# The sum of the normed residual and the gated row: VectorE in SBUF in place of TensorE in a bank

## The chip, the cores and the metric

One core of one Trainium2 chip runs the whole program in one launch. The metric is the device time of the program in microseconds; a profiled execution has a time of its own and, a little below it, the span from its first to its last record. TensorE is called PE here, VectorE DVE, ScalarE ACT, GpSimd POOL and SyncE SP.

## What is computed

Eight examples of 512 tokens by 512 features pass through two blocks of attention and feed-forward. Only the last lines of the last feed-forward and its residual matter here:

```python
for _ in range(K_STEPS):                    # 4 steps, on one row per example
    t = layer_norm(thought, pn_gamma, pn_beta)
    t = jax.nn.gelu(t @ d1_w + d1_b, approximate=False)
    thought = thought + (t @ d2_w + d2_b)
broadcast = (thought @ bc_w + bc_b)[:, None, :]
gate = jax.nn.sigmoid(x @ gate_w + gate_b)
out = x + gate * broadcast
return layer_norm(out, out_gamma, out_beta)
...
x = x + _layernorm(_L1_ffn_ref(_layernorm(x, axis=-1), ...), axis=-1)
```

The inner `x` is the layer norm of the residual: the "normed residual". `gate * broadcast` is the "gated row".

## The kernel before

Everything up to the last feed-forward runs example by example, software-pipelined over the engines, and takes the first 3705 us. For each example it leaves the residual x3 and the sigmoid gate in DRAM, and the moments of the residual in SBUF (`pd_moments`, `pd_rstd`).

The output stage takes the rest. It works on tiles of 128 tokens by 512 features, f32: `NF` = 32 tiles, four per example, in a written-out software pipeline. Each engine has its own loop, and only semaphores tie them together. `fin_place(k)` gives the two SBUF places of tile k, the residual and the gate; the second is overwritten step by step and is at last what goes out. Per tile k:

- SP loads residual and gate of a whole example (`fin_load`), three examples ahead at most.
- PE spreads the row of the example over 128 partitions of a bank (`fin_row`, L2416, once per example; banks P0, Y0, O).
- ACT makes `fin_h`, the normed residual, from residual, rstd and shift (`fin_first`, L1366), three tiles ahead; it has four places and waits for the sum of tile k - 4.
- DVE multiplies row and gate in place: the gated row (L1962).
- PE adds the two: a matmul of `fin_h` by an identity and one of the gated row by an identity into the same bank, E0 or E1 in turn (L2427, L2428). The f32 matmuls have two records each in the trace.
- DVE takes the statistics of the sum from the bank (L1944, L1949 through `fin_measure` and `fin_aggregate`), and writes (sum - mean) * gamma to SBUF (L1981).
- POOL makes rstd from the variance (L1074, L1076).
- DVE multiplies by rstd and adds beta (L1967), and takes the statistics of that (L1944, L1949).
- POOL makes the second rstd and a shift (L1074, L1076, L1088, L1090), ACT applies them in place (L1374), and POOL adds the residual (L1095). SP stores the tile (L882).

DVE's loop has `NF + 2` turns; in turn k it does the first step of tile `new` = k, the middle ones of `mid` = k - 1 and the last ones of `old` = k - 2. Its order within a turn is L1962 (new), L1967 (old), L1944 (mid), row work, L1944 (old), L1949 (mid), L1949 (old), L1981 (mid), row work. POOL's turn is rstd of one tile, rstd and shift of the one before, and L1095 of the one before that.

The rows of the first seven examples are done when the stage begins. That of the last one is not, and its four steps are woven into the first turns: `rows_work(1, p)` is called with p = 2k and 2k + 1 in turn k on DVE and PE, and nearby on ACT and POOL, and a table (`ROWS_DVE`, `ROWS_PE`) says what falls on which p. A step takes 12 of them, six turns: norm (DVE: L1737, L1742, L1744), T (PE, L2295, 8 small matmuls), "in" (DVE, L1764), d1 in two halves (PE, L2307, 16 matmuls each), "bias" (DVE, L1772), Gelu (ACT), tr (PE, L2314), "hid" (DVE, L1775), d2 in two halves (PE, L2319, 32 in all), "part" (DVE, L1778), a sum (PE, L2325), "add" (DVE: L1781, L1783, L1731, L1733), and a small rstd on POOL. PE's queue is in order: the sum of tile k stands ahead of the row work of p = 2k.

Of the kernel before, what the change touches and what calls it, by code (L numbers as in the profile page):

```python
# [5 lines left out]
ALU = mybir.AluOpType  # L6
# [299 lines left out]
def build(nc, x, raw_f, raw_i, gate_scale, up_scale, down_scale, rope1_tables, causal, identity_b,  # L306
# [8 lines left out]
    with ExitStack() as ctx:  # L315
# [15 lines left out]
        ident, k_dec = ident_dec[:, 0:P], ident_dec[:, P:P + 2 * H0].rearrange("p (c h) -> p c h", c=2)  # L331
# [10 lines left out]
        stats, moments = sb("stats", [P, NL, 6]), sb("moments", [P, NL, 2])  # L342
# [80 lines left out]
        gam, bet = X[1][:, 3, :], y_acc[:, 3, :]  # L423

        def row_const(n):
# [11 lines left out]
        fin_h = sb("fin_h", [P, 4, D], c=G)  # L437
# [5 lines left out]
        ps = {n: pairs_[n[0]][:, int(n[1]), :] if n[0] in "TE" else ctx.enter_context(nc.psum_tensor("ps_" + n, [P, 512], F32))  # L443
              for n in BANKS}
# [158 lines left out]
        NF = NB * NT  # L603
# [4 lines left out]
        fin_h_done, fin_w = count("fin_h", NF), count("fin_w", NF)  # L608
        fin_gated, fin_sum, fin_scaled, fin_affine, fin_out = (count("fin_" + k, NF) for k in ("gated", "sum", "scaled", "affine", "out"))
# [1 line left out]

        fin_moments, fin_rstd = ([Count(s_[k].sem, NF, after=NB * NT) for k in ("xa", "pa")] for s_ in (ln_moments, ln_rstd))
        fin_shift2 = count("fin_shift2", NF)
        BC_BANKS, SUM_BANKS = ("P0", "Y0", "O"), ("E0", "E1")

        def fin_place(k):

            b, t = divmod(k, NT)
            return (xr[:, t, :], y1[:, t, :]) if b == NB - 1 else tuple(fin_ring[b % FIN_RING][:, e, t, :] for e in range(2))
# [771 lines left out]
        def _(dve):  # L1391
# [549 lines left out]
            def fin_measure(k, m, src, need):  # L1941
                n = m * 4 + k % 4
                dve.wait_ge(*need)
                dve.bn_stats(stats[:, n, :], src).then_inc(*fin_stats[m].hit(k))  # L1944
# [6 lines left out]
            for k in range(NF + 2):  # L1951
                new, mid, old = k, k - 1, k - 2
                if new < NF:
                    b, t = divmod(new, NT)
                    z = fin_place(new)[1]
                    if t == 0:
                        dve.wait_ge(*fin_bc.need(b))
                        if b < NB - 1:
                            dve.wait_ge(*fin_in[b % FIN_RING].need(b // FIN_RING))
                    if b == NB - 1:  # L1960
                        dve.wait_ge(*gate_done.need(b, t))
                    dve.tensor_tensor(z, ps[BC_BANKS[b % FIN_RING]][:, :], z, ALU.mult).then_inc(*fin_gated.hit(new))  # L1962
                if 0 <= old < NF:
                    n, z = old % 4, fin_place(old)[1]
                    dve.wait_ge(*fin_scaled.need(old))
                    dve.wait_ge(*fin_rstd[0].need(old))
                    dve.scalar_tensor_tensor(z, z, rstd[:, n:n + 1], bet, ALU.mult, ALU.add).then_inc(*fin_affine.hit(old))  # L1967
                if 0 <= mid < NF:
                    fin_measure(mid, 0, ps[SUM_BANKS[mid % 2]][:, :], fin_sum.need(mid))
                if new < NF:  # L1970
                    rows_work(1, 2 * new)
                if 0 <= old < NF:
                    fin_measure(old, 1, fin_place(old)[1], fin_affine.need(old))
                if 0 <= mid < NF:
                    fin_aggregate(mid, 0)
                if 0 <= old < NF:
                    fin_aggregate(old, 1)
                if 0 <= mid < NF:
                    n, z = mid % 4, fin_place(mid)[1]
                    dve.wait_ge(*fin_moments[0].need(mid))  # L1980
                    dve.scalar_tensor_tensor(z, ps[SUM_BANKS[mid % 2]][:, :], moments[:, n, 0:1], gam, ALU.subtract, ALU.mult)\  # L1981
                        .then_inc(*fin_scaled.hit(mid))
                if new < NF:
                    rows_work(1, 2 * new + 1)

        @block.tensor
        def _(pe):
# [3 lines left out]
            def fill(bank, emptied):  # L1991

                if bank in empties:
                    pe.wait_ge(*empties[bank])
                empties[bank] = emptied
                return ps[bank]
# [333 lines left out]
            for n in range(NB + 1):  # L2330
# [44 lines left out]
                for s in range(SLOTS):  # L2375
# [8 lines left out]
                    if c >= 0:  # L2384
# [8 lines left out]
                        if 0 <= t < NT:  # L2393
# [3 lines left out]
                            dst = fill(OB[t % 2], y_copy.need(c, t))  # L2397
# [23 lines left out]
            for k in range(NF):  # L2421
                if k == NF - NT:
                    fin_row(NB - 1)
                pe.wait_ge(*fin_h_done.need(k))
                pe.wait_ge(*fin_gated.need(k))
                dst = fill(SUM_BANKS[k % 2], fin_scaled.need(k))
                pe.matmul(dst[:, :], ident[:, :], fin_h[:, k % 4, :], start=True, stop=False)  # L2427
                pe.matmul(dst[:, :], ident[:, :], fin_place(k)[1], start=False, stop=True).then_inc(*fin_sum.hit(k))  # L2428
                if k % NT == NT - 1 and k // NT + FIN_RING < NB - 1:
                    fin_row(k // NT + FIN_RING)  # L2430
                for p in (2 * k, 2 * k + 1):
                    rows_work(1, p)
# [112 lines left out]
```

## Time and profile before

| | us |
|---|---|
| median of 3 runs (lowest to highest) | 3875.98 (3874.77 to 3876.49) |
| the profiled execution | 3875.49 |
| its span | 3873.6 |
| PE busy in the span | 3614.9 (93%) |
| DVE busy | 2558.6 (66%) |
| ACT busy | 1502.3 (39%) |
| POOL busy | 1501.3 (39%) |

Shares are averages over the whole span. In the output stage, less than a twentieth of it, the balance of the engines is another one, so it has to be read by itself. A record's length runs from its start to its end; on DVE the next operation can start some 0.08 us before the end of the one before, so work is counted from start to start. An operation that is held up after it was issued shows the time in its own length, not as idle time before it.

### The profile page before, as it was taken

The numbers are of one execution on the slowest core, as the hardware profiler recorded it, in microseconds if no ns is written. First come the engines' busy times: TensorE is split into PE (matmuls) and PEld (weight loads), VectorE is DVE, ScalarE is ACT, GpSimd is POOL, SyncE is SP. The second block draws the span as 40 slices with busy tenths as digits, with TensorE's granted clock in tenths as the row PEclk, the third lists the DMA queues.
The fourth block names the chain that finished last, engine by engine and source line by source line (L and its number), as shares of the span: only waits on it lengthen the run. The fifth ranks groups of instructions, "written<-read, shape, count | busy, mean of one in ns | idle before, by whom it ended". The sixth has DMA issues, their size and how long they took to land.

```text
span 3873.6 us, 51710 instructions
## 1 busy us (share of the span) xinstructions
PE 3614.9 (93%) x18752; PEld 2656.7 (69%) x18752; DVE 2558.6 (66%) x4102; ACT 1502.3 (39%) x2327; POOL 1501.3 (39%) x1846
## 2 busy tenths in 40 slices
PE   6878999999999999999999999999999999978787
PEld 5756786687767886687767786687767786654432
DVE  6755677567764776567765776567765777467568
ACT  5523434434242534434243434344243434314323
POOL 3421562246323552245323552255223552231237
PEclk9989999999999999999999999999999999978888
DMA  6567533254324533353335433454325442350232
GB/s 248 182 223 283 193 124 142 101 216 157 131 104 171 188 116 141 127 205 136 133 108 195 164 140 117 152 187 143 139 88 211 142 159 87 120 187 23 77 112 106
DMA packets 173800, 579.03 MB, mean 149 GB/s; under 512 B 14727, under 2 KB 14983, under 8 KB 168174
## 3 DMA queue, kind: packets, MB, share of 16 engines
q1 hardware_dynamic: 169854, 568.38, 40.8%
q10 hardware_dynamic: 3696, 7.34, 0.5%
q8 instruction: 153, 2.51, 0.3%
q14 instruction: 97, 0.79, 0.1%
HBM read 490.21 MB, written 84.93 MB: 148 GB/s over the span
## 4 chain that ended last, share of the span: by engine, by line
PE 59%; DVE 23%; issue 7%; POOL 5%; ACT 3%; DMA 3%; SPq 0%; DVEq 0%; ACTq 0%; POOLq 0%
PE ps_P L2019 21%; PE ps_Y L2019 9%; PE ps_E L2019 6%; PE ps_O L2019 4%; PE ps_O L2256 4%; PE ps_T L2225 3%; PE ps_T L2019 2%; PE ps_E L2239 2%; DVE roped L1451 2%; DVE pf L1513 2%; DVE row_max L1656 2%; DVE ps_T L1649 2%; DVE stats L1417 1%; DVE roped L1445 1%; POOL X L910 1%
## 5 line engine op out<-in xcount | busy, mean ns | idle before, releaser
L2019 PE MATMUL ps_P<-XnT_hi,w_ring 128*128 128x512 f32 x3328 | 1071.4, 403 | 42.3 <-DVE hf L1676 10.7
L2019 PEld LDWEIGHTS ps_P<-XnT_hi,w_ring 128*128 128x128 f32 x3328 | 600.1, 189 | 211.6 <-issue 77.3
L2019 PE MATMUL ps_P<-XnT_lo,w_ring 128*128 128x512 f32 x1664 | 653.6, 393 | 0.0
L1036 POOL TENSOR_TENSOR hT_lo<-hf,hT_hi 128x512 fp32r<-128x512 f32 x128 | 164.8, 1287 | 871.4 <-ACT hT_hi L1100 871.4
L1252 ACT ACTIVATE probs<-ps_E 128x1024 f32<-128x1024 f32 x320 | 328.2, 1026 | 395.3 <-PE ps_E L2239 394.8
L917 POOL TENSOR_TENSOR pT_lo<-pf,pT_hi 128x512 fp32r<-128x512 f32 x256 | 346.4, 1365 | 302.4 <-ACT pT_hi L1100 302.4
L1656 DVE TENSOR_REDUCE row_max<-ps_T 128x2 fp32r<-128x768 f32 (+3 forms) x448 | 399.9, 916 | 11.0
L1649 DVE TENSOR_TENSOR ps_T<-ps_T,mask 128x512 f32<-128x512 f32 (+1 forms) x320 | 188.1, 588 | 301.3 <-PE ps_T L2225 299.5
L2019 PEld LDWEIGHTS ps_P<-XnT_lo,w_ring 128*128 128x128 f32 x1664 | 314.5, 189 | 69.8
L2019 PE MATMUL ps_Y<-w_big,hT_hi 128*128 128x512 f32 x848 | 312.8, 414 | 13.3 <-POOL hT_lo L1036 7.7
L928 POOL TENSOR_TENSOR sines<-swapped,sinT 128x512 f32<-128x512 f32 x160 | 224.8, 1405 | 172.2 <-ACT swapped L1100 166.0
L1100 ACT ACTIVATE pT_hi<-pf 128x512 fp32r<-128x512 f32 x256 | 161.5, 632 | 289.7 <-DVE pf L1513 289.5
L1100 ACT ACTIVATE swapped<-ps_P 64x512 f32<-64x512 f32 x320 | 189.8, 593 | 188.0 <-PE ps_P L2019 106.2
L972 POOL TENSOR_SCALAR_AFFINE_SELECT probs<-probs 128x512 f32<-128x512 f32 x256 | 159.6, 638 | 239.8 <-ACT probs L1252 238.9
L1513 DVE TENSOR_TENSOR pf<-ps_T,dec 128x512 f32<-128x512 f32 x256 | 172.4, 688 | 119.3 <-POOL pT_lo L917 100.6
L2019 PEld LDWEIGHTS ps_Y<-w_big,hT_hi 128*128 128x128 f32 x848 | 159.0, 187 | 81.5 <-issue 16.4
L2225 PE MATMUL ps_T<-KT,QT 64*128 64x256 f32 (+3 forms) x1024 | 164.5, 379 | 42.1 <-DVE row_max L1656 40.5
L2019 PE MATMUL ps_Y<-w_big,oT_hi 128*128 128x512 f32 x512 | 171.9, 397 | 10.7 <-DVE y_acc L1490 6.3
L1666 DVE SCALAR_TENSOR_TENSOR silu<-silu,ps_P 128x512 f32<-128x512 f32 x128 | 87.5, 684 | 141.3 <-ACT silu L1346 141.3
L1445 DVE TENSOR_TENSOR roped<-ps_P,cosT 128x512 f32<-128x512 f32 x160 | 109.7, 685 | 105.0 <-ACT swapped L1100 104.7
L1451 DVE TENSOR_TENSOR roped<-roped,sines 128x512 f32<-128x512 f32 x160 | 158.3, 990 | 24.0 <-POOL sines L928 24.0
L2019 PE MATMUL ps_O<-w_big,oT_hi 128*128 128x512 f32 x512 | 168.9, 391 | 0.0
(319 smaller groups left out, 7401.6 us busy)
## 6 DMA issues: line engine op xcount, KB each, us to landing
w_ring<-split_dram SPq DMA_DIRECT2D x412, 512.0 KB, 3.4
w_big<-split_dram SPq DMA_DIRECT2D x64, 2048.0 KB, 7.6
dec<-decay SPq DMA_DIRECT2D x32, 1024.0 KB, 5.1
split_dram<-w_ring SPq DMA_DIRECT2D x58, 512.0 KB, 4.5
split_dram<-w_big SPq DMA_DIRECT2D x36, 512.0 KB, 4.4
wo1w<-split_dram SPq DMA_DIRECT2D x8, 2048.0 KB, 7.7
gatew<-split_dram SPq DMA_DIRECT2D x7, 2048.0 KB, 11.0
X<-raw_f SPq DMA_DIRECT2D x46, 256.0 KB, 5.1
```

Of the source, the lines that this page charges most:

```text
L917: pool.tensor_tensor(pT[1][:, k % 4, :], pf[:, k % 2, :], pT[0][:, k % 4, :].bitcast(F32), ALU.subtract).then_inc(*p_lo.hit(n, g, k))
L928: pool.tensor_tensor(sines[:, u % 2, :], swapped[:, u % 2, :], sinT[:, :], ALU.mult)\
L972: pool.affine_select(out=corner, in_=corner, compare_op=ALU.is_ge, fill=0.0, base=0, pattern=[[0, 4], [1, P]], channel_multiplier=-1).then ...
L1036: pool.tensor_tensor(hT[1][:, m % IC, :], hf[:, m % 2, :], hT[0][:, m % IC, :].bitcast(F32), ALU.subtract).then_inc(*h_lo.hit(n, m))
L1100: return act.activation(out_, in_, ACT.Copy)
L1252: act.activation(dst[:, heads_of(ns), :].rearrange("p (b n) i -> p b n i", n=len(ns)), psE[:, :, :].rearrange("p b (n i) -> p b n i", n=le ...
L1451: dve.tensor_tensor(roped[:, u % 3, :], roped[:, u % 3, :], sines[:, u % 2, :], ALU.add)\
L1513: dve.tensor_tensor(out_, in_, table, ALU.mult).then_inc(*p_f.hit(n, g, pf_at(g, k)))
L1649: dve.tensor_tensor(corner.rearrange("p b n (k s) -> p b (n k) s", s=P) if nh == 1 else corner, corner.rearrange("p b n (k s) -> p b (n k) ...
L1656: last = dve.reduce_max(row_max[:, g % 2, block, heads_of(ns)].rearrange("p (b n) -> p b n", n=len(ns)), psT[:, :, at:at + len(ns) * w].re ...
L2019: last = pe.matmul(dst, stat[s_], mov[m_], start=first_ and k == 0, stop=last_ and k == n - 1, **kw)
L2225: last = pe.matmul(dst[q][:, at + m * w:at + (m + 1) * w], QT[rows_, g % 3, pair, cols(block)], KT[rows_, g % 3, 0:w], start=True, stop=True)
```

## The change

PE no longer makes the sum and has no bank for it. DVE adds `fin_h` to the gated row in place, in the same turn as L1962, behind L1967. The statistics (L1944) and L1981 read the sum from SBUF. The semaphore `fin_sum` is now raised by DVE; ACT's wait for it stays.

```diff
-        BC_BANKS, SUM_BANKS = ("P0", "Y0", "O"), ("E0", "E1")
+        BC_BANKS = ("P0", "Y0", "O")
...
                     dve.scalar_tensor_tensor(z, z, rstd[:, n:n + 1], bet, ALU.mult, ALU.add).then_inc(*fin_affine.hit(old))
+                if new < NF:
+                    dve.wait_ge(*fin_gated.need(new))
+                    dve.wait_ge(*fin_h_done.need(new))
+                    dve.tensor_tensor(fin_place(new)[1], fin_h[:, new % 4, :], fin_place(new)[1], ALU.add).then_inc(*fin_sum.hit(new))
                 if 0 <= mid < NF:
-                    fin_measure(mid, 0, ps[SUM_BANKS[mid % 2]][:, :], fin_sum.need(mid))
+                    fin_measure(mid, 0, fin_place(mid)[1], fin_sum.need(mid))
...
                     dve.wait_ge(*fin_moments[0].need(mid))
-                    dve.scalar_tensor_tensor(z, ps[SUM_BANKS[mid % 2]][:, :], moments[:, n, 0:1], gam, ALU.subtract, ALU.mult)\
+                    dve.scalar_tensor_tensor(z, z, moments[:, n, 0:1], gam, ALU.subtract, ALU.mult)\
                         .then_inc(*fin_scaled.hit(mid))
...
-                pe.wait_ge(*fin_h_done.need(k))
-                pe.wait_ge(*fin_gated.need(k))
-                dst = fill(SUM_BANKS[k % 2], fin_scaled.need(k))
-                pe.matmul(dst[:, :], ident[:, :], fin_h[:, k % 4, :], start=True, stop=False)
-                pe.matmul(dst[:, :], ident[:, :], fin_place(k)[1], start=False, stop=True).then_inc(*fin_sum.hit(k))
```

## Rows read from the trace of the kernel before

**Rows 1.** Windows: length, then PE, PEld, DVE, ACT, POOL busy; granted clock; DMA share
```profile
3705.03:3737.73 32.70, 28.74 (x108) 9.64 (x106) 22.49 (x45) 11.10 (x15) 10.23 (x26) 0.84 0.39 145
3737.73:3768.72 30.99, 26.62 (x106) 8.95 (x106) 27.08 (x54) 9.82 (x13) 19.74 (x45) 0.89 0.32 119
3768.72:3800.30 31.58, 26.73 (x104) 9.21 (x104) 27.17 (x54) 9.85 (x13) 20.15 (x45) 0.82 0.52 183
3800.30:3831.36 31.06, 27.98 (x110) 10.38 (x110) 26.55 (x53) 9.74 (x13) 19.76 (x44) 0.79 0.33 119
3831.36:3856.86 25.50, 18.07 (x38) 5.91 (x38) 24.04 (x51) 9.22 (x12) 21.77 (x49) 1.00 0.16 62
3856.86:3873.60 16.74, 1.96 (x4) 0.68 (x4) 7.85 (x17) 3.25 (x4) 13.14 (x26) 0.72 0.24 94
```

**Rows 2.** Groups of instructions, output stage, 3712 to 3858
```profile
L2427 PE MATMUL ps_E<-fin_h,ident_dec 128*128 128x512 f32 x61 | 39.2, 728 | 20.7 <-DVE fin L1962 15.6 <-DVE y L1962 4.9
L2428 PE MATMUL ps_E<-fin,ident_dec 128*128 128x512 f32 x54 | 30.1, 642 | 0.0
L1095 POOL TENSOR_TENSOR fin<-fin 128x512 f32<-128x512 f32 x27 | 35.5, 1313 | 0.0
```

**Rows 3.** Waits, output stage: who waited for whom, us in total, times, longest
```profile
DVE stats L1944 <- PE ps_E L2428: 8.3, 5, 3.1
DVE X L1772 <- PE ps_P L2307: 5.8, 4, 2.2
DVE X L1764 <- PE ps_P L2295: 5.2, 3, 4.1
DVE X L1778 <- PE ps_P L2319: 4.1, 4, 1.6
```

**Rows 4.** Timeline of DVE, one turn late in the stage (start us, us, operation)
```profile
3850.21 0.68 DVE L1962 TENSOR_TENSOR y<-ps_Y,y 128x512 f32<-128x512 f32 x1
3850.81 0.74 DVE L1967 SCALAR_TENSOR_TENSOR fin<-fin,rstd,y_acc 128x512 f32<-128x512 f32 x1
3851.47 0.69 DVE L1944 BATCH_NORM_STATS2 stats<-ps_E 128x6 f32<-128x512 f32 x1
...
3852.67 0.30 DVE L1949 BATCH_NORM_AGGREGATE moments<-stats 128x2 f32<-128x6 f32 x2
3852.89 0.73 DVE L1981 SCALAR_TENSOR_TENSOR y<-ps_E,moments,X 128x512 f32<-128x512 f32 x1
3853.54 0.68 DVE L1962 TENSOR_TENSOR y<-ps_Y,y 128x512 f32<-128x512 f32 x1
```

**Rows 5.** Source lines L1614, L1737 on DVE: durations in ns, min/median/max
```profile
L1614 DVE TENSOR_TENSOR R_q<-R_q,rb x32: 691/692/694, 578.9 to 3445.9; 128x512 f32<-128x512 f32 x32
L1737 DVE TENSOR_SCALAR rows<-thought,moments,rstd x8: 525/784/1292, 3497.9 to 3802.2; 32x512 f32<-32x512 f32 x8
```

**Rows 6.** Timeline: DVE and POOL operations that overlap, in three places
```profile
3847.49 0.74 DVE L1967 SCALAR_TENSOR_TENSOR fin<-fin,rstd,y_acc 128x512 f32<-128x512 f32 x1
3847.58 0.70 POOL L1088 TENSOR_TENSOR var_eps<-moments,rstd 128x1 f32<-128x1 f32 x1
3850.78 0.55 POOL L1076 TENSOR_TENSOR rstd<-var_eps,minus_half 128x1 f32<-128x1 f32 x1
3851.41 0.19 POOL L1088 TENSOR_TENSOR var_eps<-moments,rstd 128x1 f32<-128x1 f32 x1
1265.39 1.82 POOL L928 TENSOR_TENSOR sines<-swapped,sinT 128x512 f32<-128x512 f32 x1 [1.43 <-ACT swapped L1100]
1266.74 1.01 DVE L1393 TENSOR_TENSOR qT_lo<-roped,qT_hi 128x512 fp32r<-128x512 f32 x1
```

**Rows 7.** Windows, columns as in rows 1: PE idle, then half of d1
```profile
3766.80:3769.50 2.70, 0.00 (x1) 0.03 (x1) 2.67 (x8) 0.00 (x0) 1.82 (x6) 0.85 0.45 111
3775.70:3779.00 3.30, 3.30 (x16) 0.55 (x16) 3.30 (x8) 1.52 (x2) 2.86 (x5) 0.51 0.11 41
```

**Rows 8.** Chain that ended last: T, half of d1, d2
```profile
3773.36 1.93 PE ps_P L2295 x8
3775.65 3.53 PE ps_P L2307 x16
3788.89 3.62 PE ps_P L2319 x32
```

## The prediction

> **What bounds the kernel now.** I read the windows by stretch first, since the change touches only the output stage, the last 168 us of 3873.6. All eight examples are done there: 32 tiles of 128 tokens, 34 turns of a loop (the first makes no second or third step, the last two no first). The stretches are cut where VectorE (DVE) begins L1962 of tiles 0, 6, 12, 18, 24 and 31 [rows 1]. In the first four, each of six turns, a second thread runs: the latent rows of the last example, one step of four per stretch, alternating between DVE and TensorE (PE). What is to be seen: in stretches 2 to 4 DVE is busy 27 of 31 us and PE 27 to 28, at a granted clock of 0.79 to 0.89; neither is full, they wait for each other. In the fifth, DVE is busy 24.0 of 25.5 us. In the last only GpSimd (POOL) is dense, 13.1 us, finishing tiles. PE's large share comes from the sum that the change removes: L2427 has 39.2 us in this stage, L2428 another 30.1 [rows 2].
>
> Then the waits of the stage [rows 3]: DVE waited 8.3 us for the sum itself (L1944 behind L2428) and 15.1 us for PE in the row thread (L1772, L1764, L1778), 23.4 us together. That is all that a lighter PE could give back.
>
> Last, DVE's order of work in a turn without row work [rows 4]: L1962 0.60 us to the next start, L1967 0.66, L1944 twice, 1.20 together, the two L1949 0.22, L1981 0.65, so 3.33 us a turn. POOL's turn is as long, which will matter.
>
> **The change, part by part.**
> *PE* loses two waits and two f32 matmuls per tile, four records of some 0.6 to 0.7 us that overlap in part [rows 2], about 2 us at full clock. No DMA moves; SP's stores and loads wait for POOL's result as before, and the loads run three examples ahead. ACT's L1366 waits for the sum four tiles back, which DVE finishes sooner in the turn: nothing.
>
> *DVE* gains one add a tile. No row shows this very add; the nearest is L1614, the same size, in place, both inputs in SBUF: 0.69 us long, as L1962's 0.68 [rows 5, 4], so 0.60 us of spacing. Ends: below, 0.45, from the 0.53 us of L1737 at its fastest, another operation with one tensor input [rows 5]; above, 1.01, which an SBUF-SBUF L1393 took when POOL was in the way [rows 6]. I take 0.60, the nearest row: 32 x 0.60 = 19.2 us, and a turn of 3.93. The add waits for L1962 of its own tile, covered by L1967 between them (not in turns 0 and 1: 0.1 us), and for ACT's fin_h, three tiles ahead, except tile 0: about 0.4 us once. Queued behind it are the statistics, the row work and L1981; nobody else.
>
> *L1944 and L1981* read SBUF instead of a bank: 0.68 against 0.69 us, nothing. But L1981 now has two inputs in SBUF (the tile and gamma), as the add has. What two such inputs mean is in the rows: POOL's L1088, 0.19 us when alone, took 0.70 because it was issued while L1967 (two SBUF inputs) ran, and ended with it [rows 6]; the other way, L1393 began while POOL's L928 was in flight, ended 0.5 after it, and took 1.01 where L1614 takes 0.69 [rows 5, 6]. Whoever comes second waits. A turn has one such DVE operation now and three after the change, 1.9 us of it. Two collisions follow each turn. (i) POOL's variance L1074 is released by L1949, just when L1981 starts; it will now wait for L1981's end, so rstd comes 0.5 us later, and L1967 of the next turn, which has waited for it only in the last turns, waits about 0.2 us. (ii) POOL, pushed back, is still in L1095 (1.3 us [rows 2]) when L1981 wants to start: about 0.15 us. So 0.35 a turn where POOL is dense, 4.28 us in all; 0.2 where row work gives POOL room. The ends are nothing and the full exclusion below.
>
> *PE's clock.* PE is left with the row thread: in a period of some 35 us the transpose (T), 32 matmuls of d1, tr, 32 of d2 and a sum, 12 us at full clock. After 2.7 us with an idle PE the clock fell now, and the 16 matmuls of the first half of d1 ran at 0.51, the 1.2 GHz level: 3.53 us, and T took 1.93. d2's 32 take 3.62, the 2.4 GHz level [rows 7, 8]; they ran so because the sums kept PE busy in front of them. Without the sums PE stands still, but for tr, for some 5 us ahead of d2, so I take half speed for all three: T 1.9, d1 7.2, d2 7.2. Ends: full clock throughout, and half throughout.
> The Trainium skill, in "TensorE: Matmul & The Clock Gate" (The two states), likewise has an idle array fall back to 1.2 GHz; by that rule the half-speed case holds.
> What DVE does meanwhile: for T the second half of a turn, 1.46 us; for d1 a turn and a half and the lock waits, 6.8; for d2 (L1775 to L1778) 4.9. Waits left: T 0.8 with its hand-overs, d1 0.4 to 0.5, d2 2.3; I take 3.5 a period, as the clock may rise within one of them.
>
> **The sum by stretches [rows 1].**
> - Turns 0 to 5: now 32.7 with 10.2 idle on DVE. Work 22.5 + 3.6 adds + 1.0 locks + 0.5 first waits, T quite uncovered 2.1, d1 in short turns 1.0, d2 2.0: 32.7. Change 0.
> - Three periods: now 31.2 on average, 26.9 of it DVE's work; 26.9 + 3.6 + 1.2 + 3.5 = 35.2. Change 3 x 4.0 = +12.0.
> - Turns 24 to 30: now 25.5; 7 x 3.93 + 0.6 row work + 7 x 0.33 = 30.4. Change +4.9.
> - The end: one add, and two turns in which rstd comes 0.65 late: +1.9.
> Together +18.8. The profiled execution took 3875.49 (span 3873.6), 0.5 below the median of 3875.98; added to the median this gives 3894.8, so **3895**.
>
> **Rivals.**
> *A, the clock stays up.* T, d1 and d2 fit under DVE's work, periods are 31.7 (+0.5 each), the first stretch 29.7: -3.0 + 1.5 + 4.9 + 1.9 = +5.3, 3881. For it: PE kept 1.00 in stretch 5 with pauses of over a us between sums. Against: those pauses are short, and the 2.7 us above were enough.
> *B, full exclusion.* If every POOL operation held DVE's two-input operations off for its whole length and the reverse, a bare turn would be 3.3 + 1.9 = 5.2 instead of 4.3: 7 x 0.9 = +6.3 in stretch 5, +1.9 at the end, and about 0.3 a turn under row work where POOL has slack, +7: 3910; with half of it 3902. Against: L1967 begun 0.03 us after L1076 (0.55 us) kept its 0.74 [rows 4, 6], so short operations hold little.
> The Trainium skill, in "SBUF — State Buffer" (Who interferes with whom), has the pair locked for the whole instruction against two-SBUF-input DVE work; that is this rival, while the row on L1076 goes against its letter.
> *C, the other side: DVE's idle refills.* All 23.4 us of waits for PE [rows 3] vanish, no lock bites: 19.2 - 23.4 = -4.2, 3872 (within 0.2%); faster beyond that needs the add under 0.5 us too, 32 x 0.45 = 14.4, -9.0, 3867. It decides at a spacing of 0.73 us against 23.4 us. For it: the sum really stands in front of row work on PE (d1 is split by two sums). Against: d2's and T's waits are set by PE's own speed.
> *D, the change does not take:* excluded, the matmuls are gone from PE's code and nothing else writes the sum.
>
> **How the numbers follow.** A measurement of this kernel can tell about 0.2%, 7.8 us, from no change. Forecast case, 3889 to 3901: 0.70. A: 0.10. B: 0.14. C: 0.06. Bounds of the add's price: down 4.8; up 13 in the worst case, which is B's effect by another name. The range reaches down to the edge of A and up to the milder half of B, and leaves out C and the rest of both, some 2 in 10: 3882 to 3905. Faster 0.02, same 0.11 (A and most of C), slower 0.87.
>
> **What would show it.** DVE's L1944 never waits for PE. A bare turn between two L1962: 4.2 to 4.4 us. L1981 sometimes above 0.73, mean 0.8 or more; L1074 near 0.7 instead of 0.19; L1967 idle for POOL's rstd some 5 us in total. PE's granted clock 0.5 to 0.7 in stretches 2 to 4, d2's 32 matmuls 5 to 7 us, and L1778 waiting 1 to 2.5 us each time. Wrong if d2 stays at 3.6 us (A), if bare turns reach 5 us (B), or if bare turns stay under 4.0 and periods under 32 (C).

## The result, and the profile after

The changed kernel's median is 3893.07 us (five runs, 3889.95 to 3901.6) against 3874.77 us before (five runs, 3871.96 to 3876.49): a ratio of 1.0050, interval 1.0036 to 1.0065. That is slower, 18.3 us where 18.8 were forecast. The agreement is partly luck, as the stretches show.

The profiled execution took 3901.6 us, with a span of 3899.7. Its output stage begins at 3717.51, 12.5 us later than in the trace of before. At least 4.9 us of that is a difference between executions, since the same kernel profiled once more began it at 3712.58; what recurs is taken up below, under "The total". What can be compared is the stage itself: 182.19 us now (3899.70 - 3717.51), 182.12 in the second profile, and 168.57 before: **+13.6**.

Windows of the changed kernel, cut at L1962 of the same tiles as [rows 1], with the same columns:

```profile
3717.51:3749.14 31.63, 17.84 (x84) 5.53 (x82) 26.26 (x50) 11.12 (x15) 12.63 (x25) 0.75 0.41 149
3749.14:3783.57 34.43, 17.40 (x82) 5.29 (x82) 31.00 (x60) 9.86 (x13) 24.30 (x45) 0.70 0.30 107
3783.57:3817.71 34.14, 16.28 (x80) 5.13 (x80) 30.91 (x61) 9.72 (x13) 24.31 (x45) 0.70 0.47 169
3817.71:3851.74 34.03, 16.89 (x86) 6.61 (x86) 30.36 (x60) 9.83 (x13) 24.36 (x46) 0.70 0.30 109
3851.74:3881.20 29.46, 6.75 (x10) 1.40 (x10) 28.74 (x58) 9.23 (x12) 26.82 (x47) 0.62 0.14 53
3881.20:3899.70 18.50, 0.00 (x0) 0.00 (x0) 9.24 (x18) 3.25 (x4) 14.85 (x27) 0.50 0.22 85
```

Against [rows 1] the stretches changed by -1.1, +3.4, +2.6, +3.0, +4.0 and +1.8 (their sum is 13.6, rounding apart). In the middle three DVE is busy 30 to 31 us of 34, PE only 16 to 17, and PE's granted clock, 0.79 to 0.89 before, is 0.70. In the fifth POOL is as dense as DVE.

Waits in the output stage, as in [rows 3] (who waited for whom, us in total, times, longest):

```profile
DVE X L1778 <- PE ps_P L2323: 9.8, 4, 2.7
DVE X L1764 <- PE ps_P L2299: 4.0, 5, 2.0
DVE y L1967 <- POOL rstd L1076: 1.9, 4, 0.8
DVE fin L1967 <- POOL rstd L1076: 1.1, 6, 0.2
DVE fin L1971 <- ACT fin_h L1366: 0.4, 1, 0.4
DVE X L1772 <- PE ps_P L2311: 0.2, 1, 0.2
```

L1944's 8.3 us are gone, and so are nearly all of L1772's 5.8, but L1778, which waits for d2, went from 4.1 to 9.8. Why, PE's own timeline of one row period tells (start us, us, operation, idle time before it and its releaser):

```profile
3754.67 1.91 PE L2299 MATMUL ps_P<-ident_dec,rows 32*128 32x32 f32 x8 [12.20 <-DVE rows L1744]
3756.96 3.60 PE L2311 MATMUL ps_P<-d1w,X 128*32 128x512 f32 x16 [0.38 <-DVE X L1764]
3760.49 1.12 PE L2420 MATMUL ps_Y<-dsc,ident_dec 32*128 32x512 f32 x2
3761.54 1.92 PE L2311 MATMUL ps_P<-d1w,X 128*32 128x512 f32 x16
3764.94 0.66 PE L2318 MATMUL ps_P<-ident_dec,X 128*128 128x128 f32 x4 [1.48 <-ACT X L1271]
3768.82 6.20 PE L2323 MATMUL ps_P<-d2w,hiddenT 128*32 128x512 f32 x32 [3.23 <-DVE hiddenT L1775]
```

PE stood idle for 12.20 us before T. T and the first 16 matmuls of d1 ran at the 1.2 GHz level (1.91, 3.60), the other 16 at 2.4 GHz (1.92, as before). Then came idle stretches of 1.48 and 3.23 us around tr, and d2 took 6.20 instead of the 3.62 of [rows 8].

The same turn as in [rows 4], with POOL beside DVE:

```profile
3876.24 0.78 DVE L1985 SCALAR_TENSOR_TENSOR y<-y,moments,X 128x512 f32<-128x512 f32 x1
3876.44 0.64 POOL L1074 TENSOR_TENSOR var_eps<-moments,eps_ffn 128x1 f32<-128x1 f32 x1
...
3876.95 0.68 DVE L1962 TENSOR_TENSOR y<-ps_Y,y 128x512 f32<-128x512 f32 x1
3877.16 0.55 POOL L1076 TENSOR_TENSOR rstd<-var_eps,minus_half 128x1 f32<-128x1 f32 x1
3877.67 0.19 POOL L1074 TENSOR_TENSOR var_eps<-moments,eps 128x1 f32<-128x1 f32 x1
3877.81 0.75 DVE L1967 SCALAR_TENSOR_TENSOR y<-y,rstd,y_acc 128x512 f32<-128x512 f32 x1 [0.18 <-POOL rstd L1076]
3877.94 1.03 POOL L1076 TENSOR_TENSOR rstd<-var_eps,minus_half 128x1 f32<-128x1 f32 x1
3878.48 0.69 DVE L1971 TENSOR_TENSOR y<-fin_h,y 128x512 f32<-128x512 f32 x1
...
3879.08 1.28 DVE L1944 BATCH_NORM_STATS2 stats<-y 128x6 f32<-128x512 f32 x2
...
3879.46 1.27 POOL L1095 TENSOR_TENSOR fin<-fin 128x512 f32<-128x512 f32 x1
...
3880.49 0.78 DVE L1985 SCALAR_TENSOR_TENSOR y<-y,moments,X 128x512 f32<-128x512 f32 x1
...
3881.20 0.68 DVE L1962 TENSOR_TENSOR y<-ps_Y,y 128x512 f32<-128x512 f32 x1
```

The turn is 4.25 us (L1962 to L1962), four times in a row. DVE starts L1944 0.60 us after the add, as priced. Its own work is 3.93; the other 0.3 is L1967 waiting for POOL (0.18 and a late hand-over) and a slightly longer L1985. POOL has no idle time in it: L1074, issued while L1985 runs, takes 0.64 instead of 0.19, and L1076, issued while L1967 runs, 1.03 instead of 0.55. POOL's turn of 3.33 plus 0.45 plus 0.48 is 4.26.

### The profile page after: what moved, and what is told of

The parts are those of the page before. It is cut to its first block, busy times and chain, and to the rows that moved or that the text cites. A ratio compares the mean times of both kernels' runs of the same rounds, so it can differ in the third digit from the quotient of the medians.

```text
span 3899.7 us, 51486 instructions
## 1 busy us (share of the span) xinstructions
PE 3567.6 (91%) x18624; PEld 2641.5 (68%) x18624; DVE 2581.4 (66%) x4134; ACT 1503.1 (39%) x2327; POOL 1524.1 (39%) x1846
## 4 chain that ended last, share of the span: by engine, by line
PE 58%; DVE 23%; issue 8%; POOL 5%; DMA 3%; ACT 3%; SPq 0%; DVEq 0%; ACTq 0%; POOLq 0%
PE ps_P L2023 21%; PE ps_Y L2023 9%; PE ps_E L2023 5%; PE ps_O L2023 4%; PE ps_O L2260 4%; PE ps_T L2229 3%; PE ps_T L2023 2%; PE ps_E L2243 2%; DVE roped L1451 2%; DVE pf L1513 2%; DVE row_max L1656 2%; DVE ps_T L1649 2%; DVE stats L1417 1%; DMA w_big<-split_dram 1%; DVE roped L1445 1%
```

## Experiments

All were compared with the kernel before on the same chip. The stage is counted from the first L1962 to the end of the span, in one profile each. neither_bank and extra ran once, so their times are single values without an interval. "Difference" is the kernel's median less the median of before in the same group of runs (3876.59, 3875.59 or 3876.77 us).

| kernel | stage us | less before's 168.57 | median us (runs) | difference | ratio [interval] |
|---|---|---|---|---|---|
| again | 182.12 | +13.6 | 3894.20 (4) | +17.6 | 1.0047 [1.0032, 1.0062] |
| neither | 172.07 | +3.5 | 3883.55 (10) | +7.0 | 1.0019 [1.0010, 1.0029] |
| bank | 180.55 | +12.0 | 3891.22 (4) | +14.6 | 1.0040 [1.0025, 1.0055] |
| warm | 181.13 | +12.6 | 3891.35 (4) | +14.8 | 1.0041 [1.0026, 1.0056] |
| neither_bank | 163.02 | -5.6 | 3874.91 (1) | -0.7 | |
| keepwarm | 174.55 | +6.0 | 3885.97 (10) | +10.4 | 1.0026 [1.0017, 1.0035] |
| before_keepwarm | 163.40 | -5.2 | 3875.25 (11) | -0.3 | 0.9996 [0.9988, 1.0005] |
| hybrid | 158.51 | -10.1 | 3870.61 (11) | -5.0 | 0.9985 [0.9976, 0.9993] |
| h_bank | 179.22 | +10.7 | 3889.42 (6) | +12.7 | 1.0029 [1.0017, 1.0041] |
| extra | 193.34 | +24.8 | 3905.00 (1) | +28.2 | |
| hybrid_warm | 157.14 | -11.4 | 3868.94 (11) | -7.8 | 0.9980 [0.9971, 0.9988] |
| hybrid_zero | 160.94 | -7.6 | 3872.41 (11) | -4.4 | 0.9987 [0.9978, 0.9996] |

**again** is the changed kernel, unaltered.

> The changed kernel once more, unaltered, on the chip of the three next runs. The output stage (from the first L1962 to the end of the span) took 182.2 us in its profile and 168.6 in the kernel before, +13.6, while the medians differ by 18.3. If the change acts in the output stage alone, the stage is again 180 to 184 and whatever else differs lies before it and changes from run to run. If something ahead of the stage is slower by the change, the first L1962 is again some 12 us later than the 3705 of before.

Every stretch came out within 0.03 us of the first profile. So the stage repeats, and differences of a few tenths in it can be read.

**neither**: the sum is made by nobody. The statistics and the scaling read the gated row alone, so the normed residual is missing from the output.

```diff
-                if new < NF:
-                    dve.wait_ge(*fin_gated.need(new))
-                    dve.wait_ge(*fin_h_done.need(new))
-                    dve.tensor_tensor(fin_place(new)[1], fin_h[:, new % 4, :], fin_place(new)[1], ALU.add).then_inc(*fin_sum.hit(new))
...
-                    fin_measure(mid, 0, fin_place(mid)[1], fin_sum.need(mid))
+                    fin_measure(mid, 0, fin_place(mid)[1], fin_gated.need(mid))
```

ACT, which waited for the sum, waits for the gated row and for its own `fin_h` of the same tile.

> The sum is made by nobody: DVE's add is taken out, the statistics and L1985 read the gated row; the residual's part is missing from the output. Everything else is as in the changed kernel. Theory P (add's own DVE time is the loss, PE's speed is covered): the stage falls by 32 x 0.6 = 19 us against the changed kernel, to 163. Theory Q (the row thread on a half-speed PE and the port conflicts of L1985 set the pace, the add mostly fills time that DVE would wait): it falls by 4 to 8 us only, to 174 to 178, still longer than the 168.6 of before, and DVE waits more for L1778 and L1772.

The stage is 172.07: the add is worth 10.1 us of the 13.6, though 32 adds at 0.60 are 19.2 us of work; that lies between what the two theories gave. The surprise is in the bare turns: 4.23 us, as with the add, for 3.33 us of DVE's work. A timeline of DVE and POOL late in this stage (in this kernel the lines from L1944 on are numbered one higher, and the scaling is L1982):

```profile
3865.60 1.26 POOL L1095 TENSOR_TENSOR fin<-fin 128x512 f32<-128x512 f32 x1
...
3866.04 1.38 DVE L1982 SCALAR_TENSOR_TENSOR y<-y,moments,X 128x512 f32<-128x512 f32 x1
3866.83 0.64 POOL L1074 TENSOR_TENSOR var_eps<-moments,eps_ffn 128x1 f32<-128x1 f32 x1
...
3868.20 0.75 DVE L1968 SCALAR_TENSOR_TENSOR y<-y,rstd,y_acc 128x512 f32<-128x512 f32 x1 [0.78 <-POOL rstd L1076]
```

L1982 met L1095 in flight and took 1.38 us: it began 0.82 us before L1095's end and ended 0.56 after it, so that it lost 0.65 us to the overlap (0.73 is its length undisturbed). L1074, issued into it, ended 0.05 after it, and L1968 stood idle for 0.78. So the two-input scaling alone, with no add, brings the turn to POOL's 4.24.

**neither_bank** puts that to the test: as neither, but the scaling reads its first input from an old bank, so that one of its inputs is in SBUF. What it reads there is old content, and the residual is missing as well.

```diff
-                    dve.scalar_tensor_tensor(z, z, moments[:, n, 0:1], gam, ALU.subtract, ALU.mult)\
+                    dve.scalar_tensor_tensor(z, ps[("E0", "E1")[mid % 2]][:, :], moments[:, n, 0:1], gam, ALU.subtract, ALU.mult)\
```

> As neither (nobody makes the sum, DVE's add is out), and L1985 takes its first input from a bank with old contents, so it has one tensor in SBUF; output wrong by that too. neither had a bare turn of 4.23 us with only 3.33 us of DVE work in it, the same as with the add. Theory: that turn is set by POOL's chain, which L1985 holds up twice a turn. Then the bare turn goes back to 3.3 us, the fifth stretch from 28.5 to about 25.5, the last from 18.5 to 17, and the stage from 172.1 to about 167; the row periods change by less than 1 us. If the removed PE work were what slowed the turn, it would stay at 4.2.

The bare turn is back at 3.33 us and the stage at 163.02, 9.0 below neither: that is the price of the second SBUF input where there is no add. The rows of the same place in the turn:

```profile
3855.80 0.73 DVE L1982 SCALAR_TENSOR_TENSOR y<-ps_E,moments,X 128x512 f32<-128x512 f32 x1
3855.96 0.18 POOL L1074 TENSOR_TENSOR var_eps<-moments,eps_ffn 128x1 f32<-128x1 f32 x1
```

L1074 was issued into the scaling here too, and took 0.18. Against before, this kernel has PE's sums taken out (and the statistics read SBUF): a lighter PE gives back 5.6 us net, of the 23.4 us that DVE waited for PE before.

Net, because this kernel also pays something that the kernel before and the changed kernel do not. Once in each of stretches 2 to 5, L1968 (the affine step, two SBUF inputs) met POOL's L1095, and took 1.85 or 1.86 us where it takes 0.74: 4.5 us in all. The first of them:

```profile
3746.07 1.86 DVE L1968 SCALAR_TENSOR_TENSOR fin<-fin,rstd,y_acc 128x512 f32<-128x512 f32 x1
3746.11 1.27 POOL L1095 TENSOR_TENSOR fin<-fin 128x512 f32<-128x512 f32 x1
```

Without them PE's relief would be between 5.6 and 10.1 us; how much of the 4.5 stood on the path wasn't tried. The stage came out 4 us below the 167 expected, and the row periods gained 0.4 to 1.9 us, where less than 1 was expected.

**bank**: the add stays, but DVE writes the sum to the old banks, and the statistics and the scaling read it there. One SBUF input less for the scaling; the add keeps its two.

```diff
-                    dve.tensor_tensor(fin_place(new)[1], fin_h[:, new % 4, :], fin_place(new)[1], ALU.add).then_inc(*fin_sum.hit(new))
+                    dve.tensor_tensor(ps[("E0", "E1")[new % 2]][:, :], fin_h[:, new % 4, :], fin_place(new)[1], ALU.add).then_inc(*fin_sum.hit(new))
...
-                    dve.scalar_tensor_tensor(z, z, moments[:, n, 0:1], gam, ALU.subtract, ALU.mult)\
+                    dve.scalar_tensor_tensor(z, ps[("E0", "E1")[mid % 2]][:, :], moments[:, n, 0:1], gam, ALU.subtract, ALU.mult)\
```

> The changed kernel with DVE's sum written to a bank (E0, E1 in turn) instead of in place: the add still reads two tensors in SBUF, the statistics and L1985 read the bank, so L1985 has one tensor in SBUF. If POOL's L1074 is held by L1985's second SBUF input, its 0.64 us go back to 0.19, L1967 waits no more, a bare turn falls from 4.25 to about 3.95 us and the stage by 3 to 6 us. If it is not the port but the work itself, the turn stays at 4.25.

By source line, L1985 and L1074 (count, ns min/median/max):

```profile
L1985 DVE SCALAR_TENSOR_TENSOR y<-ps_E,moments,X x4: 733/733/734, 3871.1 to 3882.0; 128x512 f32<-128x512 f32 x4
...
L1074 POOL TENSOR_TENSOR var_eps<-moments,eps_ffn x32: 179/189/191, 3720.5 to 3882.8; 128x1 f32<-128x1 f32 x32
```

Both are at their lengths of before and the bare turn is 3.93, DVE's own work. But the stage falls by only 1.6 us where 3 to 6 were expected, 1.3 of them in the last 18.5 us, and the row periods not at all (34.41, 34.26, 34.12). In the bare turns DVE and POOL are nearly equally long, 3.93 and 4.25, so that taking the lock off L1985 can give 0.3 a turn and no more. And in each of stretches 2 to 5 a new collision appears: a DVE operation with two SBUF inputs, L1967 or the add L1971, meets L1095:

```profile
3751.41 1.87 DVE L1967 SCALAR_TENSOR_TENSOR fin<-fin,rstd,y_acc 128x512 f32<-128x512 f32 x1
3751.45 1.27 POOL L1095 TENSOR_TENSOR fin<-fin 128x512 f32<-128x512 f32 x1
...
3786.48 1.77 DVE L1971 TENSOR_TENSOR ps_E<-fin_h,fin 128x512 f32<-128x512 f32 x1
```

The four (the others begin at 3820.74 and 3847.08) are 1.1 us each over their length, 4.4 together, and the changed kernel has none of this size in these stretches. So bank trades one collision for another, and the price of the scaling's second input beside the add lies between 1.6 and 6.0 us.

**h_bank** takes the add's second SBUF input away as well: ACT writes `fin_h` to four banks, and the add works in place there; ACT waits for the scaling of tile k - 4 instead of its sum.

```diff
-                    dve.tensor_tensor(fin_place(new)[1], fin_h[:, new % 4, :], fin_place(new)[1], ALU.add).then_inc(*fin_sum.hit(new))
+                    dve.tensor_tensor(ps[("E0", "E1", "T0", "T1")[new % 4]][:, :], ps[("E0", "E1", "T0", "T1")[new % 4]][:, :], fin_place(new)[1], ALU.add).then_inc(*fin_sum.hit(new))
```

> The changed kernel with ACT writing the normed residual to four banks (E0, E1, T0, T1), DVE adding in place there, and the statistics and L1985 reading the bank: neither the add nor L1985 has two tensors in SBUF. bank, where only L1985 was freed, had a stage of 180.55 us and a bare turn of 3.93. If the add's own port use costs anything, the stage is 2 us or more under 180.55; if the rest is the add's work and PE's low clock, it is 179 to 181 and the bare turn 3.93 again.

The bare turn is 3.92 us and the stage 179.22, 1.3 us below bank. So the add's second SBUF input costs little here; most of what the add costs is its time on DVE. L1967, which still has two SBUF inputs, met L1095 three times here (1.86 or 1.87 us, 3.4 us over its length), so this kernel isn't free of the lock either.

**extra** adds a second operation of 0.6 us a tile behind the add, with one SBUF input and a result that nobody reads.

```diff
+                    dve.tensor_tensor(ps["E0"][:, :], ps["E1"][:, :], bet, ALU.mult)
```

> The changed kernel with a second DVE operation of the same length behind the add (a bank times beta, into a bank, read by nobody, one tensor in SBUF). The bare turn is 4.25 us now, 3.93 of it DVE's work. If POOL's chain sets it, the operation fills the 0.3 us of slack first: the turn becomes 4.5 to 4.6 and not 4.85, and the row periods grow by 2 to 3 us and not by 3.6, since part of the wait for d2 (9.8 us in all) is filled. Stage 191 to 197 against 182.1; 201 if every operation is paid in full.

The stage grew by 11.2 us for 19.2 us of work. In bare turns only 0.30 of 0.60 is paid (4.55), since POOL's 4.25 was longer than DVE's 3.93; under the rows part of it goes into the wait for d2, which fell from 9.8 to 5.0. So 0.6 us more of DVE's work a tile costs 0.53 of its length in this stage the first time (10.1 of 19.2) and 0.58 the second (11.2).

**warm** leaves the changed kernel as it is and gives PE back its two matmuls per tile at the old place, behind the old waits, with a constant operand, into banks that nobody reads.

```diff
+                pe.wait_ge(*fin_h_done.need(k))
+                pe.wait_ge(*fin_gated.need(k))
+                dst = fill(("E0", "E1")[k % 2], fin_scaled.need(k))
+                pe.matmul(dst[:, :], ident[:, :], bet, start=True, stop=False)
+                pe.matmul(dst[:, :], ident[:, :], bet, start=False, stop=True)
```

> The changed kernel, and PE does the two identity matmuls per tile again, with the same waits, on a constant operand into banks that nobody reads. DVE's add stays. Theory Q: granted clock back near 0.9 in stretches 2 to 4, d2's 32 matmuls 3.6 us and not 6.2, L1778's waits near nothing; the stage falls by 5 to 9 us, to 173 to 177. If PE's clock does not matter, the stage stays at 182 or grows, since the row thread is queued behind the matmuls again.

The stage is 181.13, where 173 to 177 were expected. The clock is back at 0.81 to 0.83 in the row periods and d2 at 3.64 us; its wait fell from 9.8 to 0.7. But the wait for d1 went from 0.2 to 6.3, because the two dummies stand between its halves:

```profile
3746.07 3.64 PE L2311 MATMUL ps_P<-d1w,X 128*32 128x512 f32 x16 [0.38 <-DVE X L1764]
3749.64 1.63 PE L2431 MATMUL ps_E<-y_acc,ident_dec 128*128 128x512 f32 x2
3751.11 1.02 PE L2432 MATMUL ps_E<-y_acc,ident_dec 128*128 128x512 f32 x2
3752.06 1.12 PE L2420 MATMUL ps_Y<-dsc,ident_dec 32*128 32x512 f32 x2
3753.11 1.92 PE L2311 MATMUL ps_P<-d1w,X 128*32 128x512 f32 x16
```

The dummies, like the old sums, have two effects on the row thread, a clock and a place in the queue: 9.1 us of waits gained and 6.1 lost, and the four stretches with row work are 3.0 us shorter. The fifth is 1.9 longer, so that 1.1 is left of the stage's gain. There the last spread row stands behind a tile's dummies, on a PE that is at the low level again (L2420 in 2.07 us, 1.12 at the high one), and DVE waits 1.5 us for it; right behind that, L1967 met L1095 and took 1.67 us.

**keepwarm** separates the two: dummies only where PE is idle, two ahead of T, one behind d1, two behind tr.

```diff
+                if k % 6 == 0 and k < 24:
+                    pe.wait_ge(*fin_gated.need(k))
+                    for _ in range(2):
+                        pe.matmul(fill("T0", fin_gated.need(0))[:, :], ident[:, :], bet, start=True, stop=True)
                 for p in (2 * k, 2 * k + 1):
                     rows_work(1, p)
+                    if p < 48 and p % 12 in (2, 5):
+                        for _ in range(p % 12 // 2):
+                            pe.matmul(fill("T0", fin_gated.need(0))[:, :], ident[:, :], bet, start=True, stop=True)
```

> The changed kernel, and PE does dummy matmuls only where it would stand still: two in front of each T, one behind d1, two behind tr, on a constant operand, waiting for nobody but L1962 ahead of T. If PE's clock alone makes DVE wait 9.8 us for d2 and 4.0 us for T, both waits fall to 2 us or less together, d2 takes 3.6 us, periods fall from 34.2 to 31 to 32 and the stage from 182.1 to 172 to 176. If PE's clock hides behind something else, periods stay above 33.5.

The wait for d2 is gone altogether, and the stage is 174.55, 7.6 us below the changed kernel's; the medians say 7.2 (10.4 against 17.6). The wait for T didn't fall as expected (4.1 us, and 4.0 in the changed kernel), and in one period the dummies ahead of T did not help d1 either: all 32 matmuls of d1 ran at the low level, and DVE waited 2.9 us for them. PE's timeline of that period, the second half of d1 and d2:

```profile
3751.48 3.61 PE L2311 MATMUL ps_P<-d1w,X 128*32 128x512 f32 x16
...
3760.47 3.64 PE L2323 MATMUL ps_P<-d2w,hiddenT 128*32 128x512 f32 x32 [1.51 <-DVE hiddenT L1775]
```

The dummies behind d1 and tr brought the clock up before d2 even here.

**before_keepwarm** does the same to the kernel before: two dummies in the last turn of a period, one ahead of the row work of its first.

```diff
+                if k % 6 == 5 and k < 24:
+                    for _ in range(2):
+                        pe.matmul(fill("T0", fin_gated.need(0))[:, :], ident[:, :], bet, start=True, stop=True)
+                if k % 6 == 0 and k < 24:
+                    for _ in range(1):
+                        pe.matmul(fill("T0", fin_gated.need(0))[:, :], ident[:, :], bet, start=True, stop=True)
```

> The kernel before with two dummy matmuls behind the sum of each step's last tile, and one in front of T. PE keeps 2.4 GHz over T and the first half of d1, which now run at 1.2 in three of four periods. Saved 0.9 us on each T and 1.8 us on each first half of d1, on the path of the row thread: the periods fall from 31.2 to 29 or 30, and the stage from 168.6 to 162 to 166. If the dummies delay the sums by as much, nothing is gained.

The clock in the first four stretches rose to 0.94 and the stage fell by 5.2 us to 163.40, but the time did not move: 0.9996 [0.9988, 1.0005]. So the stage's gain in one profile is not proof of a gain in time: this profile began the stage 6.6 us later than that of before (see "The total").

**hybrid** uses what the change teaches. DVE makes the sum only of tiles 1, 7, 13 and 19, those whose sums stand between the halves of d1 on PE; PE makes the other 28 as before, and the sums have a semaphore for each engine.

```diff
+        on_dve = [k for k in range(NF) if k < 24 and k % 6 == 1]
...
-                if new < NF:
+                if new < NF and new in on_dve:
...
+                if k in on_pe:
+                    pe.wait_ge(*fin_h_done.need(k))
+                    pe.wait_ge(*fin_gated.need(k))
+                    dst = fill(SUM_BANKS[k % 2], fin_scaled.need(k))
+                    pe.matmul(dst[:, :], ident[:, :], fin_h[:, k % 4, :], start=True, stop=False)
+                    pe.matmul(dst[:, :], ident[:, :], fin_place(k)[1], start=False, stop=True).then_inc(*sum_hit(k))
```

> DVE makes the sum of one tile in six (tiles 1, 7, 13, 19, the ones whose matmuls stand between the halves of d1 in PE's queue), PE the others, as before. The 8.3 us that L1944 waits for L2428 and most of the 5.8 us of L1772 fall away for four adds of 0.60 us; the stage falls from 168.6 to 160 to 166. If the row thread is late by PE's half speed anyway, the wait moves to L1772 and the stage stays within 2 us of 168.6.

PE's timeline of a period (L2316 is T, L2328 d1, L2437 the spread row, L2340 d2; sums are L2449 and L2450):

```profile
3742.16 1.07 PE L2316 MATMUL ps_P<-ident_dec,rows 32*128 32x32 f32 x8 [1.90 <-DVE rows L1761]
3743.83 3.26 PE L2328 MATMUL ps_P<-d1w,X 128*32 128x512 f32 x16 [0.59 <-DVE X L1781]
3747.02 1.12 PE L2437 MATMUL ps_Y<-dsc,ident_dec 32*128 32x512 f32 x2
3748.07 1.92 PE L2328 MATMUL ps_P<-d1w,X 128*32 128x512 f32 x16
...
3754.83 3.64 PE L2340 MATMUL ps_P<-d2w,hiddenT 128*32 128x512 f32 x32
```

No sum stands in d1 any more, d2 keeps the high level, and DVE pays four adds instead of 32. L1944's wait went from 8.3 to 1.0 and the one for d1 from 5.8 to 2.2. The stage is 158.51, below the 160 to 166 expected, and the median 5.0 us below that of before, ratio 0.9985 [0.9976, 0.9993]: small, and faster than both kernels.

**hybrid_warm** adds before_keepwarm's dummies to it, but for the first turn.

> hybrid (stage 158.5 us) with the dummy matmuls of before_keepwarm, except ahead of the first T. In hybrid the granted clock is 0.94 in stretches 2 to 4 already, so T and d1 have little left to gain: the stage is 156 to 160, and the time within 0.1% of hybrid's 3870.6. If T and d1 still started at 1.2 GHz there, it would fall by another 3 to 5 us.

The stage is 157.14, the median 3868.94, ratio 0.9980 [0.9971, 0.9988]. It is the fastest kernel of the study, but its interval overlaps hybrid's, so that the dummies help is not shown.

**hybrid_zero** lets DVE make the sum of tile 0 as well.

```diff
-        on_dve = [k for k in range(NF) if k < 24 and k % 6 == 1]
+        on_dve = [k for k in range(NF) if k == 0 or k < 24 and k % 6 == 1]
```

> hybrid with tile 0 on DVE as well. There DVE waits 4.1 us for the first T, which stands behind the matmuls of tiles 0 and 1's bank rows on PE at 1.2 GHz. Expected: the first stretch falls from 30.7 to 28 to 29.5 us (the add 0.6 and its wait for fin_h 0.4, against about 2.8 us of matmuls in front of T), the rest unchanged, the stage 156.5 to 158. If the wait for T is set by the rows and not by the queue, nothing falls and the first stretch grows by 1.

The first stretch became 2.2 us shorter (28.53 for 30.73), and the rest of the stage lost 4.6: the granted clock fell to 0.83 in two later stretches, and L1944 waited 2.7 us for a sum once. Two operations of DVE also met L1095 there (L1988 in 1.76 us, L1984 in 1.87, 2.2 us over their lengths), which happens nowhere in hybrid. That the one edit moved everything behind it against POOL and PE is a reading, and wasn't tested; the tile alone is not worth it. The intervals of the two kernels overlap.

## Why the prediction held, and where it didn't

**The sum by stretches.**

| | predicted | measured |
|---|---|---|
| turns 0 to 5 | 0 | -1.1 |
| three row periods | +12.0 (35.2 each) | +9.0 (34.43, 34.14, 34.03) |
| turns 24 to 30 | +4.9 (30.4) | +4.0 (29.46) |
| the end | +1.9 | +1.8 |
| stage | +18.8 | +13.6 |

**Right.** The add is 0.68 us long with a spacing of 0.60. L1944 never waits for PE. The clock falls: PE's granted clock is 0.70 in the row periods, d2 takes 6.2 us, and DVE waits 9.8 / 4 = 2.45 us for it, predicted 2.3; for T 0.5 to 1.0 a period, predicted 0.8. The bare turn is 4.25, predicted 4.28, by the chain named: L1985 holds up L1074, and rstd comes late. The end came as computed.

**Right by errors that cancel: the wait for d2.** The prediction set d2 at 7.2 us against 4.9 of DVE's work. In the period shown it took 6.20, since only part of it ran at the low level. But it began 0.72 us after L1775 and L1778 came 0.08 after its end, which the prediction left out, and DVE had 4.63 us of work to do from L1775 to L1778: 0.72 + 6.20 + 0.08 - 4.63 = 2.37.

**Mis-sized: the locks under row work.** The step "0.2 where row work gives POOL room", 1.2 us a period, measured less. A period of 34.2 on average, less the 26.9 of work, the 3.6 of adds and 3.1 of waits for T and d2, leaves 0.6. L1967 waited 3.0 us for rstd in all, predicted some 5, and 1.9 of these in the last turns; under row work it waited 0.2 us once in a period. Bank doesn't settle the price, as its own collisions fall into the periods.

**Mis-sized: the wait for d1.** Predicted 0.4 to 0.5 a period, measured 0.2 in the whole stage. d1 was to run at half speed throughout (7.2); the clock rose within it (3.60 and 1.92 above, 5.16 for all 32 in the next two periods), a case that the prediction had allowed for but not priced. In the first stretch too d1 was taken as waited for (1.0), and was not.

**Near, but for another reason: L1985.** Its mean is 0.78 us, where 0.8 or more was to be seen: 0.76 for the 28 rows of `fin`, 0.93 for the last four. Step (ii) took 0.15 us a turn for its meeting L1095; it was 0.05 (0.78 against 0.73). The add makes the turn so long that L1095 is nearly over when L1985 starts. The full price, 1.38, is paid once in the changed kernel, in the last turns, and every bare turn only in neither. Instead L1076 was held up by L1967 (1.03 for 0.55), a collision that the prediction did not list: the right total of a bare turn has one wrong part in it.

**What the runs add** is where the 13.6 come from. Step by step from before: PE's sums out -5.6 (neither_bank), the second SBUF input of the scaling +9.0 (neither), the add +10.1. In the other order the add alone is worth +17.5 (bank less neither_bank) and the second input +1.6. Neither order is the true one: in turns without row work the length is the greater of DVE's 3.93 and POOL's 4.25, and whichever comes second is nearly free. Nor are the steps clean: neither_bank and bank hold some 4.5 us of meetings with L1095 that before, neither and the changed kernel lack or have elsewhere, which goes into the -5.6, the +9.0 and the +1.6, and cancels in the +17.5. The low clock costs the changed kernel at least 7.6 us (keepwarm, where the wait for T stayed and one d1 ran at the low level). The add cannot be bought off by a bank (h_bank), but it can be made for four tiles only (hybrid).

**The total.** The time moved by 18.3, the stage by 13.6. That 4.7 was not in the prediction, and it filled the gap that the oversized terms left. The same is seen in all twelve kernels: the difference of the medians is 2.0 to 5.1 us above the difference of the stages, also in before_keepwarm, whose program for the first 3700 us is that of before. Matched operation by operation with before, the changed kernel is 6.2 us late at 2230 us (again 1.6, so this part differs between executions), and 12.5 at the start of the stage (again 7.6): some 6 us come in between, in both profiles, and at two places.

Of the first, the window behind it in the kernel before (columns as above):

```profile
2283.00:2286.40 3.40, 3.40 (x16) 2.81 (x16) 2.71 (x4) 0.00 (x0) 2.72 (x4) 1.00 0.00 0
```

The same part of the program, to 0.4 us, in the changed kernel:

```profile
2290.00:2293.40 3.40, 3.40 (x10) 2.65 (x10) 0.57 (x2) 0.00 (x0) 1.44 (x2) 0.61 0.00 0
```

Just ahead of it PE waits 1.5 us for a load of weights (0.3 before), and its granted clock is then 0.61, where it was 1.00: 10 matmuls instead of 16 in 3.4 us. 2.8 us are lost in all, also in again and bank, about 1 or less in h_bank, keepwarm, before_keepwarm and extra, and 0.2 or less in neither, neither_bank, warm and the hybrids.

The second place is the stretch from DVE's L1624 at 3507.40 us to the stage, in before and in the changed kernel:

```profile
3507.40:3705.03 197.63, 158.39 (x1019) 85.64 (x1020) 113.19 (x186) 73.03 (x93) 40.46 (x73) 0.85 0.11 38
3516.51:3717.51 201.00, 162.68 (x1019) 87.82 (x1020) 113.43 (x186) 73.19 (x93) 40.49 (x73) 0.83 0.11 38
```

The same 1019 matmuls keep PE busy for 4.3 us longer, at a lower granted clock, and the stretch is 3.4 us longer. It is 3.2 to 3.4 longer in nine of the thirteen profiles besides that of before (before_keepwarm is one: 201.00, at 0.83), and within 0.1 of before in neither_bank and the three hybrids. So a kernel whose program ahead of the stage is unchanged can lose 3.4 us there, and the change itself isn't needed for it.

Why the load lands later and why the clock falls in an unchanged part of the program was not tried. Nor do the two places give the offset of each kernel: hybrid has neither, and its medians still differ by 5.1 us more than the stages. As before was profiled in one execution only, it can't be excluded that its stage or its first part was unusual. So 13.6 of the 18.3 us are seen in the stage; 4.7 lie ahead of it or between executions, and their cause stays open.

**The rivals.** A (the clock stays up) fell: 0.70, d2 at 6.2; keepwarm, where d2 kept 3.64 us, comes near what it would have given, a stage 7.6 shorter: +6.0 on before, and A had said +5.3. B (full exclusion) fell for this kernel, with the bare turn at 4.25 and not 5.2. But it is no fiction: in a handful of meetings a DVE operation with two SBUF inputs was held by the 1.3 us L1095 and ended 0.5 to 0.6 us after it: 1.38 us instead of 0.73 in neither, 1.85 to 1.87 instead of 0.74 in neither_bank, bank and h_bank, and 1.77 instead of 0.69 for the add. The reverse is there too: in bank L1095, begun 0.05 us behind L1967, took 1.83 us instead of 1.27, and L1967 kept its 0.74. The changed kernel mostly escapes by its timing, since the longer turn lets L1095 nearly finish before L1985. The Trainium skill, in "SBUF — State Buffer" (Who interferes with whom), says that the shared ports are an exclusive lock, that a DVE instruction with two SBUF inputs contends for them with a GpSimd instruction that reads SBUF, and that the issue order decides who blocks. L1982's 1.38 us against L1095 agree, and so do L1074's 0.64 and L1076's 1.03 here. Two rows don't fit the part on order: the short L1076 of [rows 6], already in flight, did not hold L1967 up, and L1967 in bank, whose record begins 0.04 us before L1095's, was held all the same. C (DVE's idle time refills) fell: PE's relief gave 5.6 us, at most 10.1, and not 23.4, since d2's wait grew as the clock fell (4.1 us before, 7.9 in neither_bank). Its seed, the sum between the halves of d1, is what hybrid lives on.

## What to carry to other kernels

Before taking work off an engine, ask what the work did for its neighbours in the queue: PE's sums here kept its clock up for the row thread (worth at least 7.6 us) and at four places delayed it, so moving only those four beat moving all 32. When an operand moves from a bank to SBUF, count the SBUF inputs of every DVE operation that reads it, and follow a POOL engine that shares the turn: where two loops are of nearly equal length, taking a cost off one of them shows almost nothing. List the lengths of single operations before reading a kernel that takes one cost away: in bank and neither_bank a few meetings with a long POOL operation, 1.1 us each, blur what the edit shows. And when the stage that was changed gains 5 us in a trace, measure the time all the same.

## Not expected of the hardware

- A POOL operation of one element a partition, issued while a DVE operation with two SBUF inputs ran, ended after it: L1074 0.64 us instead of 0.19, L1076 1.03 instead of 0.55, which is L1967's end plus 0.41. With one of the inputs in a bank, the same L1074, issued at the same point, took 0.18.
- The same scaling took 0.73, 0.78 or 1.38 us, by where its inputs were and what POOL had in flight, and L1967, begun 0.04 us before POOL's L1095 by its record, 1.87 instead of 0.74.
- Within one pass of d1 the clock rose from the 1.2 to the 2.4 GHz level (16 matmuls in 3.60 us, the next 16 in 1.92), and idle stretches of 1.48 and 3.23 us behind it, with 0.66 us of work between them, brought it back down for part of d2: 6.20 us, between the 3.62 of one level and the 7.2 of the other.
